# Attention slots regrouped by output batch, with the division of the results moved into attention (decoder layer, fp32, one core)

## The chip, the cores and the metric

The kernel runs on one core of a Trainium2 chip. The metric is the device time of one execution in microseconds (us). The core has five engines with a queue each: TensorE (PE in the rows; its weight loads are PEld), VectorE (DVE), ScalarE (ACT), GpSimd (POOL) and SyncE (SP), which here issues all DMA transfers. Sixteen DMA engines carry them. TensorE's clock has two levels, 2.4 GHz (1.0 in the rows) and 1.2 GHz (0.5).

## The reference

Three post-normalised blocks on x of shape (4, 1024, 512). Only the first is touched by the change:

```python
q = _lin(_lin(x, wq_w, wq_b), vq_w, vq_b)      # k and v likewise
q = q.reshape(b, s, hc, H).transpose(2, 0, 1, 3)   # 32 heads of width 16
scores = jnp.einsum('cbqh,cbkh->cbqk', q, k) / scale
attn = jax.nn.softmax(scores, axis=-1)
o = jnp.einsum('cbqk,cbkh->cbqh', attn, v)
o = o.reshape(H, b, s, hc).transpose(1, 2, 0, 3).reshape(b, s, f)
x = _layernorm(x + _lin(o, wo_w, wo_b))
# then: x = _layernorm(x + gated_cell(conv1d(x), ctx)); x = _layernorm(x + ternary_linear(round(x)))
```

The reshape of o is a reinterpretation of memory, not a transposition back. Head c and input batch b land in output batch 2 * (c % 2) + b // 2. One output batch is therefore made of the sixteen heads of one parity and two of the four input batches, and it is complete only when all sixteen are done.

## The kernel before

All matrix products but two are made of fp32r pairs: a value is split into a high part (a cast) and a low part (value minus high part), and `product3` (L140) adds hi*hi, hi*lo and lo*hi.

**combine** (L36) multiplies the two stacked weight matrices of q, k and v. **project** (L152) goes over 8 blocks of 512 columns of x. A block has 8 tiles of q and k (128 features x 512) and 4 tiles of v. For a q/k tile ScalarE writes the high part, VectorE the low part into one of four `parts` buffers, and SyncE stores both with one DMA of 512 KB to `qk_scr` (L177). v stays in `v_sb`.

**attend** (L258) has 64 slots. A slot is one head with two input batches: `cp` counts pairs of heads, `lo` picks the head of the pair, `beta` the two batches. Per slot TensorE makes two kinds of score products. The first kind (`s1_lane`, L372) gives scores of 128 queries x 1024 keys, of which VectorE takes the row maximum (L486); there are 16 such units in a slot. GpSimd splits the maxima in two parts (`split_max`, L521, L523), and SyncE writes them as two extra rows into the q operand (`store_max`, L320). The second kind (`s2`, L391) gives transposed scores with the maximum already subtracted; ScalarE takes the exponential (L466), and `pv` (L400) multiplies by v with a column of ones beside it, so that sums come out with the results. ScalarE copies the finished slot out of PSUM (`evacuate`, L455), one copy per slot. The maxima of slot s+2 are made during slot s; before slot 0 there are 32 units of maxima alone. In the last two slots there are none.

The operands `qop` and `kop` have two buffers for a head, each with both `beta` halves. `load_op` (L301) fills a half with ten DMAs: for each of two lanes one q copy of 256 KB whose source is `broadcast_to([2, DH, 2 * S])` (L308), one of 128 KB (L310) and three k copies of 64 KB (L313). SyncE issues it when slot s has used the half, and slot s+2 needs it at its start. After it SyncE stores results and sums of the slot, eight small DMAs (L353, L356).

**finish** (L561) begins with sums of batch 0: load, reciprocal on VectorE (L1118), store, and then eight chunks of 128 features, each loaded with the reciprocals spread over its rows (L699, L702), divided by VectorE (`divide`, L1133), its high part made by ScalarE (L935) and its low part by VectorE (L1137). Then come the output projection (`wo_stage`), and for each batch a `turn` of four m steps, each of four gates with 24 convolution matmuls. The next batch's chunks are loaded, divided and split during the turn. GpSimd adds `wo_b` to x tiles (L850), makes the low parts of the convolution weights (L845) and the inverse deviations, in a fixed order. Each stage is a block of its own: the next starts when every queue, SyncE's too, has come to its end.

The order on every engine is the order in which the code is written; there is no scheduler.

Of the kernel before, what the change touches and what calls it, by code (L numbers as in the profile page):

```python
# [8 lines left out]
F32 = mybir.dt.float32  # L9
# [18 lines left out]
VW = 2 * DH  # L28
EPS = 1e-5
# [122 lines left out]
def project(nc, mem, x, x_t, w_hi, w_lo, qk_bias, v_bias, qk_scr, v_sb):  # L152
# [3 lines left out]
    with ExitStack() as ctx:  # L156
# [11 lines left out]
        bank = mem["banks"]  # L168
        with nc.Block() as block:
            @block.sync  # L170
            def _(sp):
                def blocks(it, more):
                    for i in range(2):
                        for j in range(2 * KC):

                            sp.wait_ge(qk_lo, (it * 2 + i) * (2 * KC) + j + 9)
# [3 lines left out]
                        if more:  # L180

                            sp.wait_ge(x_made, it * 2 + i + 1)
                            load_x_block(sp, x, x_t, i, it * (2 * HALF) + (i + 2) * HALF)

                with sp.Fori(0, BLK // 2 - 1) as it:
                    blocks(it, True)
                blocks(BLK // 2 - 1, False)
                for i in range(4):
                    sp.wait_ge(stored[i], DMA * (BLK * 2 + 1))
# [30 lines left out]
            def _(act):  # L220
                act.sem_inc(qk_lo, 8)  # L221
                with act.Fori(0, BLK // 2) as it:
                    for i in range(2):
                        for j in range(2 * KC):
                            act.wait_ge(proj, (it * 2 + i) * GROUPS + j + 1)
                            act.wait_ge(stored[j % 4], ((it * 2 + i) * 2 + j // 4 + 1) * DMA)
# [4 lines left out]
            def _(dve):  # L231
# [4 lines left out]
                def block_of(it, i, more):  # L236
                    for j in range(2 * KC):
                        dve.wait_ge(qk_hi, (it * 2 + i) * (2 * KC) + j + 1)
# [3 lines left out]
                    for j in range(2 * KC, GROUPS):  # L242
                        dve.wait_ge(proj, (it * 2 + i) * GROUPS + j + 1)
                        nc.vector.tensor_tensor(
                            v_sb[:, bass.ds(it * (2 * KC) + (i * KC + j - 2 * KC), 1), :].rearrange("p a f -> p (a f)"),
                            bank[6 + j % 2], v_bias[:], ALU.add).then_inc(v_out, 1)
                    if more:

                        split_x_block(nc, dve, x, i, it * 2 + i + 2, it * DMA + 2 * DMA)

                with dve.Fori(0, BLK // 2 - 1) as it:
                    for i in range(2):
                        block_of(it, i, True)
                for i in range(2):
                    block_of(BLK // 2 - 1, i, False)


def attend(nc, mem, qk_scr, v_sb, o_scr, d_scr):  # L258

# [8 lines left out]
    DEEP = 4  # L268
    with ExitStack() as ctx:
        sb = lambda name, shape, dt: ctx.enter_context(nc.sbuf_tensor(name, shape, dt))  # L270
        sem = lambda name: ctx.enter_context(nc.semaphore(name))
        qop = [sb(f"q_op{i}", [P, B, S], F32R) for i in range(2)]
        kop = [sb(f"k_op{i}", [P, B, HALF], F32R) for i in range(2)]
        vop = [sb(f"v_op{i}", [P, B * QT, VW], F32) for i in range(2)]
        probs = [sb(f"probs{i}", [P, TILES, HALF], F32) for i in range(DEEP)]
        u = [sb(f"out{i}", [P, HALF], F32) for i in range(2)]
        mx = [sb(f"neg_max{b}", [P, QT], F32) for b in range(B)]
        mparts = [[sb(f"neg_max_parts{i}{b}", [P, PARTS, QT], F32R) for b in range(B)] for i in range(2)]
# [3 lines left out]
        pv_bank = bank[7]  # L282

        op_in = [[sem(f"op_in{i}{beta}") for beta in range(2)] for i in range(2)]
        max_in = [[sem(f"max_in{i}{b}") for b in range(B)] for i in range(2)]
# [11 lines left out]
        u_stored = [sem(f"u_stored{i}") for i in range(2)]  # L297

        LAST = HEADS // 2 - 1

        def load_op(sp, head, i, beta):  # L301
            cols = slice(beta * 2 * S, (beta + 1) * 2 * S)
            rows = bass.ds(head * DH, DH)
            bs = slice(2 * beta, 2 * beta + 2)
            s = op_in[i][beta]
            for lane in range(2):
                r0 = LANE * lane
                sp.dma_start(qop[i][r0:r0 + 2 * DH, bs, :].bitcast(F32),  # L308
                             qk_scr[0, 0:1, rows, cols].broadcast_to([2, DH, 2 * S])).then_inc(s, DMA)
                sp.dma_start(qop[i][r0 + 2 * DH:r0 + 3 * DH, bs, :].bitcast(F32), qk_scr[0, 1, rows, cols]).then_inc(s, DMA)  # L310
                for r, part in enumerate((0, 1, 0)):
                    k = qk_scr[1, part, rows, cols].rearrange("r (b l n) -> r b l n", b=2, l=2)[:, :, lane, :]
                    sp.dma_start(kop[i][r0 + r * DH:r0 + (r + 1) * DH, bs, :].bitcast(F32), k).then_inc(s, DMA)  # L313
        OPS = 10 * DMA

        def store_max(sp, i, b):
            for lane in range(2):
                for part in range(PARTS):
                    r = LANE * lane + ROWS + part
                    sp.dma_start(qop[i][r:r + 1, b, :].bitcast(F32),  # L320
                                 mparts[i][b][:, part, :].bitcast(F32)).then_inc(max_in[i][b], DMA)
        MAXES = 2 * PARTS * DMA
# [1010 lines left out]
```

## Time and profile before

| | us |
|---|---|
| median of 3 runs (lowest, highest) | 2441.18 (2429.57, 2443.71) |
| profiled execution, its own time | 2461.73 |
| its span | 2460.0 |
| TensorE busy | 2247.7 (91%) |
| VectorE busy | 1703.3 (69%) |
| ScalarE busy | 1397.9 (57%) |
| GpSimd busy | 431.2 (18%) |
| mean granted clock of TensorE | 0.931 |

The page divides the span in 40 slices of 61.5 us. Projection lies in slices 1 to 5, attention in slices 6 to 29, the last stage in slices 30 to 39. TensorE's busy time is no measure of need: matmuls overlap in it and its length depends on the clock. So the rows to read are those that show a wait, a clock or a place on the time line.

### The profile page before, as it was taken

How to read it: one execution, taken by the hardware profiler on the slowest of the kernel's cores; microseconds unless marked ns; L12 is line 12 of the kernel's file. 1: busy time of each engine (PE TensorE's matmuls, PEld its weight loads, DVE VectorE, ACT ScalarE, POOL GpSimd, SP SyncE). 2: the span in 40 equal slices, each digit the busy share in tenths (PEclk: the TensorE clock that was granted, in tenths of full speed). 3: DMA queues.
4: the chain of work that ended last, by engine and by line, in shares of the span. 5: the costliest groups of instructions: out<-in, count | busy, mean ns of one | idle time of the engine just before them, and what ended most of it. 6: DMA issues, size and time to landing. Idle time of an engine off the chain costs nothing. (4 is left out here: it accounts for less than half of the span.)

```text
span 2460.0 us, 41952 instructions
## 1 busy us (share of the span) xinstructions
PE 2247.7 (91%) x11688; PEld 1273.4 (52%) x11688; DVE 1703.3 (69%) x1742; ACT 1397.9 (57%) x2534; POOL 431.2 (18%) x814
## 2 busy tenths in 40 slices
PE   8999966999999999999999999999974989989896
PEld 4688843444444444444444444444413767766663
DVE  3333327888888888888888888888704666757565
ACT  0111101777787778777777777778742544444343
POOL 0000000000000000000000000000003575665754
PEclk9899985999999999999999999999957999999998
DMA  3344431222222222222222222222106544535331
GB/s 141 112 153 162 153 98 49 57 61 61 65 63 63 57 60 66 65 64 64 56 63 62 61 61 60 60 63 64 33 23 206 175 149 135 182 124 167 103 123 48
DMA packets 174858, 223.42 MB, mean 91 GB/s; under 512 B 93264, under 2 KB 94288, under 8 KB 168656
## 3 DMA queue, kind: packets, MB, share of 16 engines
q1 hardware_dynamic: 174800, 222.70, 31.2%
q8 instruction: 30, 0.49, 0.1%
q14 instruction: 28, 0.23, 0.0%
HBM read 169.12 MB, written 51.38 MB: 90 GB/s over the span
## 5 line engine op out<-in xcount | busy, mean ns | idle before, releaser
L486 DVE TENSOR_REDUCE neg_max<-psum 128x1 f32<-128x1024 f32 x1024 | 1204.7, 1219 | 214.9 <-PE psum L372 214.5
L466 ACT ACTIVATE probs<-psum 128x512 f32<-128x512 f32 x2048 | 1066.2, 605 | 409.2 <-PE psum L391 403.8
L391 PE MATMUL psum<-q_op,k_op 50*128 50x512 f32 x2048 | 776.6, 467 | 42.4 <-DMA k_op<-qk_parts_dram 29.9
L391 PEld LDWEIGHTS psum<-q_op,k_op 50*128 50x128 f32 x2048 | 362.3, 199 | 649.6 <-ACT probs L466 563.6
L372 PE MATMUL psum<-k_op,q_op 48*128 48x512 f32 x2048 | 641.0, 497 | 36.2 <-DMA k_op<-qk_parts_dram 26.3
L400 PE MATMUL psum<-probs,v_op 128*32 128x512 f32 x4096 | 574.0, 634 | 0.1
L372 PEld LDWEIGHTS psum<-k_op,q_op 48*128 48x128 f32 x2048 | 390.1, 316 | 70.2 <-issue 27.6
L521 POOL CAST neg_max_parts<-neg_max 128x8 fp32r<-128x8 f32 x128 | 24.3, 190 | 1271.2 <-DVE neg_max L486 1271.2
L147 PE MATMUL psum<-x_hi,conv_w_hi 128*128 128x512 f32 x512 | 210.1, 410 | 7.6 <-DVE x_lo L1141 7.6
L147 PE MATMUL psum<-x_lo,conv_w_hi 128*128 128x512 f32 x512 | 204.6, 400 | 0.0
L147 PE MATMUL psum<-x_hi,conv_w_lo 128*128 128x512 f32 x512 | 204.5, 399 | 0.0
L845 POOL TENSOR_TENSOR conv_w_lo<-conv_w_raw,conv_w_hi 128x1024 fp32r<-128x1024 f32 x64 | 153.6, 2402 | 115.2 <-ACT conv_w_hi L931 114.9
L400 PEld LDWEIGHTS psum<-probs,v_op 128*32 128x32 f32 x4096 | 82.1, 109 | 133.9 <-issue 58.0
L227 ACT ACTIVATE qk_parts<-psum,qk_bias 128x512 fp32r<-128x512 f32 x64 | 44.0, 688 | 166.1 <-PE psum L147 166.0
L239 DVE SCALAR_TENSOR_TENSOR qk_parts<-psum,qk_bias,qk_parts 128x512 fp32r<-128x512 f32 x64 | 48.1, 751 | 119.9 <-ACT qk_parts L227 119.9
L939 ACT ACTIVATE x<-y,neg_mean_rstd,rstd 128x512 f32<-128x512 f32 x64 | 52.2, 816 | 138.0 <-POOL neg_mean_rstd L840 138.0
L147 PEld LDWEIGHTS psum<-x_hi,conv_w_hi 128*128 128x128 f32 x512 | 99.1, 193 | 33.5 <-DVE x_lo L1141 8.8
L147 PEld LDWEIGHTS psum<-x_lo,conv_w_hi 128*128 128x128 f32 x512 | 99.0, 193 | 22.9
L1194 DVE TENSOR_TENSOR gate_in<-psum,gate_in 128x512 f32<-128x512 f32 x64 | 44.1, 690 | 95.5 <-PE psum L147 95.2
L147 PEld LDWEIGHTS psum<-x_hi,conv_w_lo 128*128 128x128 f32 x512 | 97.8, 191 | 23.2
L147 PE MATMUL psum<-x_hi,w_hi 128*128 128x512 f32 x256 | 102.2, 399 | 5.0 <-ACTq L221 5.0
L147 PE MATMUL psum<-x_lo,w_hi 128*128 128x512 f32 x256 | 101.9, 398 | 0.0
(96 smaller groups left out, 1809.1 us busy)
## 6 DMA issues: line engine op xcount, KB each, us to landing
qk_parts_dram<-qk_parts SPq DMA_DIRECT2D x64, 512.0 KB, 2.8
q_op<-qk_parts_dram SPq DMA_DIRECT2D x128, 256.0 KB
conv_w_raw<-in_conv_w_dram SPq DMA_DIRECT2D x64, 512.0 KB, 3.3
k_op<-qk_parts_dram SPq DMA_DIRECT2D x384, 64.0 KB
q_op<-qk_parts_dram SPq DMA_DIRECT2D x128, 128.0 KB
gate_in<-in_ctx_dram SPq DMA_DIRECT2D x64, 256.0 KB, 3.6
x_block<-in_x_t_dram SPq DMA_DIRECT2D x8, 1024.0 KB, 5.8
q_op<-neg_max_parts SPq DMA_DIRECT2D x512, 4.0 KB, 2.3
```

What stands on the lines that cost most here:

```text
L147: mm = nc.tensor.matmul(out, left, right, start=(first and i == 0), stop=(last and i == n - 1))
L227: nc.scalar.activation(parts[j % 4][:, 0, :], bank[j % 6], ACT.Identity, bias=qk_bias[:, j // KC, j % KC:j % KC + 1]).then_inc(qk_hi, 1)
L239: nc.vector.scalar_tensor_tensor(out=parts[j % 4][:, 1, :], in0=bank[j % 6], scalar=qk_bias[:, j // KC, j % KC:j % KC + 1], in1=parts[j % ...
L372: return nc.tensor.matmul(s1_bank[t % 2][:, lane * HALF:(lane + 1) * HALF], qop[i][r, b, t:S:QT], kop[i][r, b, :], start=True, stop=True)
L391: nc.tensor.matmul(s2_bank[cell % RING], kop[lo][r, b, n // 2 * P:(n // 2 + 1) * P], qop[lo][r, b, j % 2 * HALF:(j % 2 + 1) * HALF], start ...
L400: mm = nc.tensor.matmul(pv_bank[32 * j:32 * j + 32, :], vop[k // 2][:, (2 * (k % 2) + j // 2) * QT + kt, :], probs[n % DEEP][:, j, :], sta ...
L466: nc.scalar.activation(probs[n % DEEP][:, j, :], s2_bank[cell % RING], ACT.Exp, scale=SCALE).then_inc(exp_done, 1)
L486: nc.vector.tensor_reduce(mx[b][:, t:t + 1], s1_bank[t % 2][:], AX_X, ALU.max, negate=True).then_inc(maxed, 1)
L521: nc.gpsimd.tensor_copy(out[:, 0, :], m[:]).then_inc(split_step, 1)
L845: G.tensor_tensor(cwl[i % 4][:], raw[i % 2][:], cwh[i % 4][:].bitcast(F32), ALU.subtract).then_inc(w_lo, 1)
L939: A.activation(dst, y[r][:], ACT.Identity, bias=nmr[:, r:r + 1], scale=rstd[:, r:r + 1]).then_inc(normed, 1)
L1194: V.tensor_tensor(gin[g][:], bank[2 + g], gin[g][:], ALU.add).then_inc(gate_in, 1)
```

## The change

- Slots are numbered by output batch: slot s is head parity and half of the batches s // 16, head pair s % 16. The weights are permuted on the way in (`by_parity`), and v is stored in slot order.
- `project` writes q and k rows as the operands need them, the doubled part twice: three DMAs of 256 KB for a tile, each 8 slots x 16 rows x 512.
- `attend` has four operand buffers of one slot each. `load_op` is four DMAs of 48 rows. The load for slot s+3 is issued at the start of slot s and first needed in the middle of slot s+1. Maxima run 24 units ahead, not 32, and there are two buffers of them, not four.
- Results are stored with one DMA a slot. For every pair of slots SyncE loads sums and results back, VectorE makes the reciprocals, SyncE stores them and loads them spread over the rows, and GpSimd multiplies, casts and subtracts (`normalise`); SyncE stores the two parts.
- In the last slot SyncE loads the output projection weights and the 16 tiles of batch 0, high and low. They lie over `v_sb`. `finish` has only the last pair to divide. The tiles of later batches are loaded ready-made during the turns.

```diff
-                            sp.dma_start(
-                                qk_scr[j // KC, :, (j % KC) * P:(j % KC + 1) * P, bass.ds(it * (2 * HALF) + i * HALF, HALF)]
-                                .rearrange("a f n -> f a n"), parts[j % 4][:].bitcast(F32)).then_inc(stored[j % 4], DMA)
...
+                        for r, part in enumerate((0, 0, 1) if j < KC else (0, 1, 0)):
+                            sp.dma_start(rows[:, r, :, :], parts[j % 4][:, part, :].bitcast(F32))\
+                                .then_inc(stored[j % 4], DMA)
...
+            q = qk_scr[0, bass.ds(s * ROWS, ROWS), :].rearrange("r (b n) -> r b n", b=2)
+            k = qk_scr[1, bass.ds(s * ROWS, ROWS), :].rearrange("r (b l n) -> r b l n", b=2, l=2)
             for lane in range(2):
-                r0 = LANE * lane
-                sp.dma_start(qop[i][r0:r0 + 2 * DH, bs, :].bitcast(F32),
-                             qk_scr[0, 0:1, rows, cols].broadcast_to([2, DH, 2 * S])).then_inc(s, DMA)
...
+                rows = slice(LANE * lane, LANE * lane + ROWS)
+                sp.dma_start(qop[i][rows, :, :].bitcast(F32), q).then_inc(op_in[i], DMA)
+                sp.dma_start(kop[i][rows, :, :].bitcast(F32), k[:, :, lane, :]).then_inc(op_in[i], DMA)
...
+                    if k % 2 == 1 and not (first and k == 1):
+                        normalise(pool, nc, norm, it * 2 + (k - 3) // 2)
+                    if not (last and k >= 2):
+                        split_max((k + 2) % 4, 0, s * 2 + 4, s * 16 + LEAD + 16, it * MAXES + MAXES + DMA)
...
+def load_pair(sp, norm, us_scr, t):
+
+    for i in range(2):
+        sp.wait_ge(norm["u_stored"][i], (t + 1) * DMA + DMA)
+    sp.sem_inc(norm["waited"], 1)
+    rows = us_scr.rearrange("s (j r) n -> (s j) r n", r=VW)[bass.ds(t * 8, 8), :, :]
+    sp.dma_start(norm["sums"][:], rows[:, DH:DH + 1, :].rearrange("a o (h m) -> a (o h) m", m=VW))\
+        .then_inc(norm["sums_in"], DMA)
+    sp.wait_ge(norm["lo_made"], t + 1)
+    sp.sem_inc(norm["waited"], 1)
+    sp.dma_start(norm["o"][:], rows[:, 0:DH, :]).then_inc(norm["o_in"], DMA)
...
+def normalise(pool, nc, norm, t):
+
+    pool.wait_ge(norm["o_in"], t * (2 * DMA) + 2 * DMA)
+    nc.gpsimd.tensor_tensor(norm["o"][:], norm["o"][:], norm["den"][:], ALU.mult).then_inc(norm["o_made"], 1)
...
+def load_o(sp, late, on_scr, b, n):
+
+    i, c = n // KC, n % KC
+    for part, dst in enumerate((late["o_hi"], late["o_lo"])):
+        src = on_scr[part].rearrange("(h l q) n -> h l q n", l=2, q=VW)[bass.ds(b * 16 + c * 4, 4), i, :, :]
+        sp.dma_start(dst[:, n, :].bitcast(F32), src).then_inc(late["o_in"][i], DMA)
...
-                            if g == 2 and m < KC - 1 and not last:
-                                for n in (2 * m + 2, 2 * m + 3):
-                                    next_o(b + 1, n)
+                            if g == 2 and not last:
+                                for n in (2 * m, 2 * m + 1):
+                                    load_o(sp, late, on_scr, b + 1, n)
```

How the queues change at three places. SyncE in the projection, two q/k tiles, before:

```order
39 L177 ISA
40 L177 DMA qk_parts_dram<-qk_parts 128x2x512
41 L176 REGISTER_ALU
42 L177 ISA
43 L177 DMA qk_parts_dram<-qk_parts 128x2x512
```

and after:

```order
34 L187 DMA qk_parts_dram<-qk_parts 8x16x512
35 L187 DMA qk_parts_dram<-qk_parts 8x16x512 x2
36 L187 DMA qk_parts_dram<-qk_parts 8x16x512
37 L187 DMA qk_parts_dram<-qk_parts 8x16x512 x2
...
```

One store for a tile has become three, and their first dimension is 8.

SyncE in the loop of attention, one operand load (`q_op`, `k_op`) with what follows it, before:

```order
125 L308 ISA
126 L308 DMA q_op<-qk_parts_dram 32x1x2048
127 L310 ISA
128 L310 DMA q_op<-qk_parts_dram 16x2048
129 L313 ISA
130 L313 DMA k_op<-qk_parts_dram 16x2x512
131 L313 ISA
132 L313 DMA k_op<-qk_parts_dram 16x2x512 x2
133 L308 DMA q_op<-qk_parts_dram 32x1x2048
134 L310 DMA q_op<-qk_parts_dram 16x2048
```

and after, in a slot that also stores the two parts and reads the next pair back (`attended_dram` holds results with their sums):

```order
...
117 L306 ISA
118 L306 DMA q_op<-qk_parts_dram 48x2048
119 L307 ISA
120 L307 DMA k_op<-qk_parts_dram 48x2x512
121 L306 DMA q_op<-qk_parts_dram 48x2048
122 L307 ISA
123 L307 DMA k_op<-qk_parts_dram 48x2x512
124 L338 ISA
125 L313 DMA q_op<-neg_max_parts 1x128x8 x4
```

The copies of 32, 16 and 16 rows are one of 48 rows, and they stand ahead of the maxima of the next slot, no longer behind both of them.

GpSimd in the loop of attention, from one split of maxima to the next, before:

```order
46 L521 CAST neg_max_parts<-neg_max 128x8
47 L522 REGISTER_ALU
48 L523 TENSOR_TENSOR neg_max_parts<-neg_max,neg_max_parts 128x8
49 L516 ISA
50 L521 CAST neg_max_parts<-neg_max 128x8
51 L522 REGISTER_ALU
52 L523 TENSOR_TENSOR neg_max_parts<-neg_max,neg_max_parts 128x8
```

and after:

```order
55 L535 CAST neg_max_parts<-neg_max 128x8
56 L536 ISA
57 L537 TENSOR_TENSOR neg_max_parts<-neg_max,neg_max_parts 128x8
58 L617 ISA
59 L618 TENSOR_TENSOR o_raw<-o_raw,recips 128x512
60 L620 ISA
61 L622 CAST o_parts<-o_raw 128x512
62 L624 TENSOR_TENSOR o_parts<-o_raw,o_parts 128x512
63 L530 REGISTER_ALU
64 L535 CAST neg_max_parts<-neg_max 128x8
```

The three wide operations stand between two splits in every second slot.

## Rows read from the trace of the kernel before

**Rows 1.** The page's 40 slices: TensorE busy, its clock (tenths), DMA share.
```profile
PE   8999966999999999999999999999974989989896
...
PEclk9899985999999999999999999999957999999998
DMA  3344431222222222222222222222106544535331
```

**Rows 2.** Waits of TensorE, 400 to 1760 us: total us, times, longest.
```profile
PE psum L391 <- DMA k_op<-qk_parts_dram: 29.9, 32, 1.6
```

**Rows 3.** Time line of ScalarE, copies of slots 0, 27, 28, 61 and 63.
```profile
441.73 0.58 ACT L455 COPY out<-psum 128x512 f32<-128x512 f32 x1
...
1030.91 0.58 ACT L455 COPY out<-psum 128x512 f32<-128x512 f32 x1
...
1051.82 0.58 ACT L455 COPY out<-psum 128x512 f32<-128x512 f32 x1
...
1773.93 0.58 ACT L455 COPY out<-psum 128x512 f32<-128x512 f32 x1
...
1835.18 0.58 ACT L455 COPY out<-psum 128x512 f32<-128x512 f32 x1 [3.00 <-PE psum L400]
```

**Rows 4.** Stretches: busy PE, PEld, DVE, ACT, POOL; clock, DMA share, GB/s.
```profile
1327.00:1335.00 8.00, 6.39 (x34) 2.71 (x32) 4.82 (x5) 4.24 (x8) 0.39 (x2) 0.73 0.12 25
1030.90:1051.80 20.90, 20.90 (x130) 9.62 (x128) 18.84 (x17) 17.00 (x34) 0.79 (x4) 1.00 0.26 65
```

**Rows 5.** Stretches for the DMA engines, columns as in rows 4.
```profile
204.00:206.00 2.00, 2.00 (x10) 1.64 (x9) 0.69 (x1) 0.00 (x0) 0.00 (x0) 1.00 1.03 386
903.00:909.00 6.00, 6.00 (x41) 3.06 (x39) 5.28 (x5) 4.82 (x11) 0.00 (x0) 1.00 0.56 122
...
915.00:918.00 3.00, 3.00 (x21) 1.37 (x24) 2.74 (x3) 2.45 (x6) 0.00 (x0) 1.00 0.13 55
```

**Rows 6.** Time line, projection's first store and entry into attention.
```profile
81.65 1.77 SPq L177 DMA_DIRECT2D qk_parts_dram<-qk_parts  x2
...
346.19 1.76 DVE L479 MEMSET k_op<- 128x2048 f32 x1 [0.89 <-PEq L169]
...
366.94 4.48 SPq L313 DMA_DIRECT2D k_op<-qk_parts_dram  x3
370.84 1.25 PE L372 MATMUL psum<-k_op,q_op 48*128 48x512 f32 x4 [26.27 <-DMA k_op<-qk_parts_dram]
...
371.70 36.29 DVE L486 TENSOR_REDUCE neg_max<-psum 128x1 f32<-128x1024 f32 x32 [20.52 <-PE psum L372]
...
413.32 0.76 PE L391 MATMUL psum<-q_op,k_op 50*128 50x512 f32 x1 [6.73 <-DMA q_op<-neg_max_parts]
```

**Rows 7.** Groups by line, VectorE: busy us, mean ns, idle before.
```profile
L1229 DVE RECIPROCAL x_int<-x_int 128x256 f32<-128x256 f32 x3 | 5.0, 1713 | 0.0
```

**Rows 8.** VectorE's reductions, line 486: ns, lowest, median, highest.
```profile
L486 DVE TENSOR_REDUCE neg_max<-psum x1024: 1209/1216/1226, 371.7 to 1769.6; 128x1 f32<-128x1024 f32 x171
```

**Rows 9.** Stretch of the last two slots, columns as in rows 4.
```profile
1774.00:1835.00 61.00, 57.29 (x185) 14.58 (x185) 0.00 (x0) 31.49 (x62) 0.00 (x0) 0.50 0.02 5
```

**Rows 10.** Time line, GpSimd and TensorE at the start of the last stage.
```profile
1882.02 4.76 POOL L845 TENSOR_TENSOR conv_w_lo<-conv_w_raw,conv_w_hi 128x1024 fp32r<-128x1024 f32 x2 [23.91 <-ACT conv_w_hi L931]
1886.73 0.20 POOL L903 COPY x<-z0s 128x8 f32<-128x8 f32 x1
...
1907.50 0.80 PE L147 MATMUL psum<-x_hi,conv_w_hi 128*128 128x512 f32 x1 [7.63 <-DVE x_lo L1141]
```

**Rows 11.** Last stage: a wait, two groups, one DMA issue (median us to landing).
```profile
PE psum L1048 <- ACT x_int_t L949: 57.0, 11, 11.4
...
L1133 DVE TENSOR_TENSOR o_raw<-o_raw,recips 128x512 f32<-128x512 f32 x24 | 15.4, 683 | 0.0
...
L935 ACT CAST o_hi<-o_raw 128x512 fp32r<-128x512 f32 x24 | 13.5, 609 | 0.0
...
x_wo<-in_x_dram SPq DMA_DIRECT2D x20, 256.0 KB, 2.7
```

More of the change, by code:

```diff
@@ L360, in _ @@
+                for k in range(4):
+                    slot(0, k, first=True)
+                with sp.Fori(1, LAST) as it:
                     for k in range(4):
-                        slot(cp, k, True)
+                        slot(it, k)
                 for k in range(4):
-                    slot(LAST, k, False)
-                for i in range(2):
-                    sp.wait_ge(u_stored[i], HEADS * 8 * DMA + DMA)
-            U_STORE = 8 * DMA
+                    slot(LAST, k, last=True)
@@ L414, in slot @@
                             unit = 2 * n + half
+                            ahead = k + 1 if unit < QT else k + 2
                             for side in range(2):
@@ L502, in _, with slot @@
-                with dve.Fori(0, LAST) as cp:
-                    for k in range(4):
-                        slot(cp, k)
-                for k in range(2):
-                    slot(LAST, k)
+                for n in range(LEAD):
+                    if n == 16:
+                        dve.wait_ge(split, 1)
+                    maxima(n // QT % 2, n % QT, n)
+                def slot(it, k, first=False, units=16):
+                    s = it * 4 + k
+                    for n in range(units):
+                        if n % QT == 0:
+                            dve.wait_ge(split, s * 2 + n // QT + 2)
+                        if n == 2 and k % 2 == 1 and not (first and k == 1):
+                            recips(dve, nc, norm, it * 2 + (k - 3) // 2)
+                        maxima(1 - n // QT, n % QT, s * 16 + n + LEAD)
@@ new lines, in _ @@
+                for k in range(4):
+                    slot(0, k, first=True)
+                with dve.Fori(1, LAST) as it:
+                    for k in range(4):
+                        slot(it, k)
+                slot(LAST, 0)
+                slot(LAST, 1)
+                slot(LAST, 2, units=QT)
+                recips(dve, nc, norm, PAIRS - 2)
+                dve.wait_ge(late["wo_in"], DMA)
+                nc.vector.tensor_copy(late["wo_hi"][:], late["x2"][:, 0:KC, :]).then_inc(late["wo_hi_made"], 1)
@@ new lines, in _, with store_out @@
+                for k in range(4):
+                    slot(0, k, first=True)
+                with pool.Fori(1, LAST) as it:
+                    for k in range(4):
+                        slot(it, k)
+                for k in range(4):
+                    slot(LAST, k, last=True)
+def store_out(sp, norm, us_scr, s, i):
+    sp.dma_start(us_scr[bass.ds(s, 1), :, :].rearrange("s p n -> p (s n)"), norm["u"][i][:])\
+        .then_inc(norm["u_stored"][i], DMA)
+def load_pair(sp, norm, us_scr, t):
+    for i in range(2):
+        sp.wait_ge(norm["u_stored"][i], (t + 1) * DMA + DMA)
[6 more added lines that the diff above has]
+    sp.dma_start(norm["o"][:], rows[:, 0:DH, :]).then_inc(norm["o_in"], DMA)
@@ L775, in turn @@
                         if m == 0 and not last:
-                            for n in range(2):
-                                next_o(b + 1, n)
+                            sp.wait_ge(row_full, wo_row(b, first) + TT)
+                            sp.wait_ge(norm["parts_stored"], (PAIRS + 1) * DMA)
+                            sp.sem_inc(waited, 1)
                         if not first:
@@ L987, in turn @@
                                 A.activation(tc[:], cell[:], ACT.Tanh).then_inc(tanh_made, 1)
-                            if g == 2 and not last:
-                                for j in range(2):
-                                    hi_o(b + 1, 2 * m + j)
                             if g == 2 and m < KC - 1 and not first:
@@ L1198, in turn @@
                                     rounded(b, 2 * m - 2 + j, before + j)
-                            if g == 1 and not last:
-                                for j in range(2):
-                                    divide(b + 1, 2 * m + j)
                             if g == 2:
```

481 lines of the change are left out of this document (232 added, 249 removed).

## The prediction

> **What bounds the kernel now.** I read the page's slices first: TensorE is busy nearly everywhere, so I look for where its clock is low and where it is empty. [rows 1] show two such places, around slice 6 (entry into attention) and slices 29 and 30 (from attention to the last stage), and small dents in the clock all through attention. Next the waits of TensorE inside attention: 30 waits, 29.9 us, for k_op [rows 2]. What they do to a slot is seen from ScalarE's copy of the result, one in each of the 64 slots: two successive copies lie 20.91 us apart where nothing was waited for, but the first and the 62nd lie 1332.2 us apart, 21.84 us a slot [rows 3]. So 61 slots lose 0.93 us each, 57 us: 30 are the waits themselves, the rest is the half clock that follows a wait, as at 1327 to 1335 us, where the granted clock averages 0.73, against 1.00 in the undisturbed slot [rows 4].
>
> Why the load is late shows in the DMA share. While many transfers run, the 16 engines are busy at 1.03 with 386 GB/s; in the tail of each operand load the share is 0.13 with 55 GB/s [rows 5]. 0.13 of 16 is two engines. The tail is the q copy whose source is written with a leading dimension of 2. From these two ends (leading dimension 2: two engines; 128: all) I take it that **a transfer gets as many engines as its leading dimension has steps**, at 386/16 = 24.1 GB/s each, and that they are always the same first ones. The sum rests on this: the change removes the leading 2, but adds transfers with a leading 8 and 4.
>
> The Trainium skill (DMA: Bandwidth & Descriptors, Why a DMA increments its semaphore by 16 and not by 1) gives the same as a rule: the largest number up to 16 that divides the slowest dimension of both sides, on the lowest-numbered engines. It speaks against two of the new transfers; the trace agrees at leading dimension 2 and has no clean stretch for 8 or 4.
>
> **The change, part by part** (against the profiled execution, 2461.73 us, span 2460.0).
>
> *Projection.* Each of 64 q/k tiles is now stored three times 256 KB, as 8x16x512, instead of once 512 KB over 128 partitions. On eight engines (193 GB/s) 0.786 MB take 4.07 us; TensorE makes 96 tiles, 32 of them v tiles that are not stored, in the 264.5 us from the first store to the next stage, 2.8 us each. So stores set the pace: 64 x 4.07 = 261 us plus six x blocks of 1 MB at 2.7 us is 277 us. The first store is at 81.65, so the last lands near 361, where attention began at 346.19 [rows 6]: **+14 us**. Bounds: 0 if all 16 engines serve them (131 us, hidden), +25 if a crowded engine is slower than 24.1 GB/s.
>
> *Entry into attention.* Before, 67.1 us pass from 346.19 to the first score matmul of the second kind (413.32); the first one of the first kind waits until 370.84, and SyncE itself is held up in issuing (4.48 us for three small DMAs) because two engines have a queue [rows 6]. Now one operand set is 1.18 MB in four transfers of 48 rows, three sets 3.5 MB, 9 us at 386 GB/s. Memsets and the first landing take about 6 us, then 24 units of maxima instead of 32, at 36.29/32 = 1.13 us: 27.1 us. 33 instead of 67: **-34 us**. The maxima of slot 0 are stored by unit 20, so that last wait goes too. Bounds -25 and -36.
>
> *Steady slots.* A load (3 us on 16 engines) now has one and a half slots, 31 us, so both the waits and the dents behind them go: -57. New in the slots: every second slot a reciprocal of 32 columns on VectorE (256 columns took 1.71 us [rows 7], so about 0.3; VectorE idles 0.25 us a pair of units, part shows): +3. GpSimd's three 128x512 operations, some 3.5 us, lie in the 10 us between two splits of maxima; VectorE's reduction reads PSUM and varies only from 1209 to 1226 ns [rows 8] with GpSimd's copies beside it, so I charge nothing for them. VectorE has now two maxima buffers, not four: it waits for a split made half a slot earlier. **-54 us**, bounds -10 and -57.
>
> *Last slots.* Without maxima the clock falls to 0.50 and the last two slots take 61.2 us [rows 3, 9]. Half a slot of that runs at full rate now, 10.5 instead of 15.3: **-5 us**.
>
> *Seam.* Before: 71.7 us from the last copy's end (1835.76) to the first convolution matmul at 1907.50 [rows 3, 10]. Now output projection weights and all of batch 0 are requested in slot 63, about 24 us before attention ends. But these are 16 transfers of 256 KB with leading dimension 4: 4.19 MB on four engines (96.5 GB/s) are 43.5 us, with the weights 46. SyncE can hardly run ahead of its queue (the 4.48 us above), so its last store and the end of the stage come some 22 us after TensorE is done: the early load is only half early. In the next stage: sums of the last pair issued after eight DMAs and landed (9 us), reciprocal, store, recips load (to 15 us), GpSimd's three operations (to 19), two conv_w_lo at 2.4 (to 24). From that point, where GpSimd copies z0, it was 20.8 us to the convolution [rows 10]; constants now go ahead of it, so 18. Together 22 + 42 = 64 against 71.7: **-7 us**. Bounds: -28 (loads on all engines) and +25.
>
> *Last stage.* VectorE loses 24 divisions and 24 subtractions of 0.7 us, ScalarE 24 copies of 0.61 [rows 11]. In turn 0 they were under the convolution; in turns 1 and 2 part of the 57.0 us that TensorE waits for ScalarE's x_int_t goes, but the large ones (the longest 11.4 us) follow the output projection, which GpSimd paces. I take -6 (bounds 0 and -15). Against it: four loads per m step, 1.05 MB on four engines, 10.9 us. At the end of a turn x tile 4 queues behind them; landed 2.7 us after its issue before [rows 11], it comes about 5 us late, and GpSimd must add it before it goes on. Three turns: +15. **+9 us**, bounds -10 and +40.
>
> Sum: 14 - 34 - 54 - 5 - 7 + 9 = **-77 us**, 2385 in the profiled frame. The profiled run is 20.5 us above the median of 2441.18. If all of that were waits for loads, unprofiled runs have less to regain, -57; I take the middle, -66: **2375 us**, own range 2340 to 2410.
>
> **Rivals.**
> *B, the other dimension decides and the loads spread.* All these transfers have 128 partitions on one side. For it: a full share at most times; against it: the 0.13 tail. Then projection +0, seam -28, last stage -6: 50 us less, 2325.
> *C, the wait moves.* GpSimd's division waits for the reciprocals on its queue ahead of the next split of maxima, and that split holds VectorE and then TensorE. Its chain (store, sums, reciprocal, store, load, each 2 to 3 us) has to end by about 17 us of the slot; I find it at 11 to 15. If it misses, every second slot loses more than 1 us and the clock dents with it, and 44 of the 54 stay: 2419.
> *D, slower.* The engines do less than 24.1 GB/s each when transfers mix. At 903 to 909 us it is 122 GB/s at a share of 0.56, 13.6 GB/s per busy engine [rows 5]. Then batch 0 needs 77 us (+34), and an m step (96 convolution matmuls at 0.22 us, 21 us in turn 0, some 29 in the later turns with the ternary product and its waits) needs 19.3 for its four loads, 9.6 for weights and 4.8 for ctx on the first four engines, 34 in all: +52 in turn 0, +44 in turns 1 and 2, less the 9 already counted: 2496. It decides from about 17 GB/s per engine downwards. Against it: those are 2 KB and 8 KB pieces crowded on two engines, not an even load.
>
> **How the numbers follow.** Forecast 0.57, B 0.13, C 0.17, D 0.08, other mishaps 0.05. The predicted time is the forecast's. The range 2312 to 2430 takes in B and C and leaves out D. One per cent (24 us) is about what a measurement can tell from no change: faster by more holds the forecast, B and half of C, 0.78; the rest of C and a bit of each, 0.12; slower D and mishaps, 0.10.
>
> **What would show it.** Right: no wait for k_op in attention, copies 20.9 to 21.0 us apart, first score matmul of attention some 6 us after the stage's start; q/k stores at a share near 0.5 without pauses up to 360; in the last slot and after it a share near 0.25, TensorE idle some 65 us; GpSimd waiting for x tiles at each end of a turn. Wrong: a share near 1 in those stretches (B); VectorE or TensorE waiting for GpSimd's splits every second slot (C); TensorE waiting for conv_w or o_hi inside the turns (D).

## The result, and the profile after

The changed kernel takes 2476.51 us (median of 4 runs, 2471.38 to 2478.00) beside 2439.53 for the kernel before (2429.57 to 2443.71). The ratio is 1.0154, 95% interval [1.0119, 1.0189]: slower by 1.5%, where 2375 was forecast. The profiled execution took 2477.05 us with a span of 2475.3; before, the span was 2460.0. The spans differ by 15.3 us and the medians by 37.0, because the profiled execution before (2461.73) lay 22 us above its median. The table splits the 15.3 us, a sum of large amounts of both signs; the forecast in the same frame was -77. The stretches end at the same rows in both traces:

| stretch, us | before | after | difference | forecast |
|---|---|---|---|---|
| start to attention's first memset | 346.2 | 399.2 | +53.0 | +14 |
| to the first score matmul of the second kind | 67.1 | 37.1 | -30.0 | -34 |
| to the first copy of a result | 28.4 | 27.1 | -1.3 | |
| first to 62nd copy | 1332.2 | 1281.1 | -51.1 | -54 |
| 62nd to last copy | 61.2 | 49.3 | -11.9 | -5 |
| last copy's start to the first convolution matmul | 61.7 | 52.9 | -8.8 | -7 |
| to the end | 563.1 | 628.6 | +65.5 | +9 |

One bound has to be put right. The prediction took the matmul at 1907.50 in [rows 10] for the first of the convolution. It is the first behind a gap; twelve stand ahead of it. TensorE's time line of the kernel before, where they begin:

```profile
1896.67 0.39 PE L147 MATMUL psum<-wo_hi,o_lo 128*128 128x512 f32 x1
1896.90 0.40 PE L147 MATMUL psum<-x_hi,conv_w_hi 128*128 128x512 f32 x1
```

and the same place after:

```profile
1846.70 0.77 PE L149 MATMUL psum<-x_hi,conv_w_hi 128*128 128x512 f32 x1 [11.73 <-DVE x_lo L1158]
```

So the seam before was some 61 us long, not 71.7. The table uses 1896.90.

**What went as forecast.** TensorE waits for no k_op in attention's slots any more, and the copies stand 1281.1 us / 61 = 21.00 us apart. ScalarE's time line, copies 1, 62 and 64, against [rows 3]:

```profile
463.37 0.58 ACT L457 COPY out<-psum 128x512 f32<-128x512 f32 x1
...
1744.46 0.58 ACT L457 COPY out<-psum 128x512 f32<-128x512 f32 x1
...
1793.79 0.59 ACT L457 COPY out<-psum 128x512 f32<-128x512 f32 x1 [2.60 <-PE psum L403]
```

**What did not: the projection.** Before, TensorE was never held there behind the first store. The groups of waits from 80 to 400 us after (in each row: who waits, for whom, us in total, times, longest):

```profile
DVE qk_parts L245 <- ACT qk_parts L232: 134.1, 40, 7.4
ACT qk_parts L232 <- DMA qk_parts_dram<-qk_parts: 111.1, 27, 10.8
...
DVE x_hi L136 <- DMA x_block<-in_x_t_dram: 47.1, 6, 10.5
PE psum L149 <- DVE values L251: 35.0, 6, 8.5
```

The stores do run on eight DMA engines: busy share 0.53 and 204 GB/s in a stretch of stores alone, 25.5 GB/s an engine, so a q/k tile of 0.786 MB takes 3.85 us. But a little later the DMA engines carry nothing at all (share 0.00). Windows (columns as in [rows 4]):

```profile
310.00:318.00 8.00, 7.60 (x23) 6.05 (x24) 1.63 (x3) 0.00 (x0) 0.00 (x0) 0.67 0.53 204
...
326.00:330.00 4.00, 4.00 (x19) 3.22 (x18) 3.44 (x3) 1.02 (x2) 0.00 (x0) 1.00 0.00 1
```

The time line of SyncE and of VectorE from the last stores of one block to the first of the next shows why:

```profile
313.39 4.85 SPq L187 DMA_DIRECT2D qk_parts_dram<-qk_parts  x4
318.29 1.14 SPq L129 DMA_DIRECT2D x_block<-in_x_t_dram  x1
330.77 3.30 SPq L187 DMA_DIRECT2D qk_parts_dram<-qk_parts  x4
```

```profile
326.52 1.23 DVE L136 CAST x_hi<-x_block 128x2048 fp32r<-128x2048 f32 x1 [7.36 <-DMA x_block<-in_x_t_dram]
327.79 2.29 DVE L138 TENSOR_TENSOR x_lo<-x_block,x_hi 128x2048 fp32r<-128x2048 f32 x1
330.00 2.72 DVE L245 SCALAR_TENSOR_TENSOR qk_parts<-psum,qk_bias,qk_parts 128x512 fp32r<-128x512 f32 x4
```

The x block load is issued behind the block's last store (318.29), VectorE waits for it (326.52), splits it, and only then makes the low part that the next store needs (330.77). A round takes 41.4 us; TensorE needs 33.6 for a block. Before the change a round took just these 33.6 us, as SyncE's x block loads show:

```profile
201.26 0.39 SPq L127 DMA_DIRECT2D x_block<-in_x_t_dram  x1
...
234.90 0.39 SPq L127 DMA_DIRECT2D x_block<-in_x_t_dram  x1
```

**And the last stage.** Waits from 1846 us to the end, after the change:

```profile
POOL conv_w_lo L884 <- ACT conv_w_hi L971: 134.6, 26, 13.0
...
ACT conv_w_hi L971 <- DMA conv_w_raw<-in_conv_w_dram: 51.3, 9, 10.0
...
PE psum L149 <- DMA o_lo<-attended_parts_dram: 48.2, 3, 23.1
```

In the kernel before, ScalarE waited 0.5 us in all for these weights (from 1896 us to the end):

```profile
ACT conv_w_hi L931 <- DMA conv_w_raw<-in_conv_w_dram: 0.5, 1, 0.5
```

SyncE's time line after the change around the four new loads of an m step:

```profile
1880.00 0.33 SPq L775 DMA_DIRECT2D conv_w_raw<-in_conv_w_dram  x1
1880.37 0.57 SPq L633 DMA_DIRECT2D o_hi<-attended_parts_dram  x1
1880.99 0.55 SPq L633 DMA_DIRECT2D o_lo<-attended_parts_dram  x1
1881.58 0.54 SPq L633 DMA_DIRECT2D o_hi<-attended_parts_dram  x1
1882.16 0.56 SPq L633 DMA_DIRECT2D o_lo<-attended_parts_dram  x1
1882.77 3.17 SPq L771 DMA_DIRECT2D gate_in<-in_ctx_dram  x1
1885.99 0.58 SPq L775 DMA_DIRECT2D conv_w_raw<-in_conv_w_dram  x1
```

Ctx and weights are issued behind the burst, and SyncE itself is held 3.17 us at the ctx load. At the end of turn 0 TensorE stands idle for the last of them, at half clock, with some four engines busy (0.28 of 16) and 101 GB/s. The three waits for `o_lo`, one at the end of each turn, come to 48.2 us, beside the 65.5 lost. Its time line and a window of that stretch:

```profile
1987.70 0.80 PE L149 MATMUL psum<-wo_hi,o_hi 128*128 128x512 f32 x1 [23.07 <-DMA o_lo<-attended_parts_dram]
```

```profile
1982.00:1987.00 5.00, 0.00 (x0) 0.00 (x0) 1.57 (x3) 1.43 (x2) 0.05 (x1) 0.50 0.28 101
```

### The profile page after: what moved, and what is told of

It reads as the page before. It is cut to its first block, busy times and chain, and to the rows that moved or that the text cites. A ratio compares the mean times of both kernels' runs of the same rounds, so it can differ in the third digit from the quotient of the medians.

```text
span 2475.3 us, 40345 instructions
## 1 busy us (share of the span) xinstructions
PE 2235.3 (90%) x11688; PEld 1280.1 (52%) x11688; DVE 1676.5 (68%) x1709; ACT 1378.2 (56%) x2501; POOL 524.2 (21%) x942
## 2 busy tenths in 40 slices
DMA packets 204432, 281.64 MB, mean 114 GB/s; under 512 B 95441, under 2 KB 95441, under 8 KB 198225
## 4 chain that ended last, share of the span: by engine, by line
PE 58%; issue 8%; POOL 7%; DMA 4%; DVE 3%; SPq 2%; ACT 1%; POOLq 0%; DVEq 0%; ACTq 0%
PE psum L394 23%; PE psum L403 20%; PE psum L376 10%; PE psum L149 4%; POOL conv_w_lo L884 3%; DMA conv_w_raw<-in_conv_w_dram 2%; SPq L633 2%; POOL rstd L877 1%; DVE neg_max L488 1%; POOL x L894 1%; DMA x_wo<-in_x_dram 1%; PE psum L1077 1%; POOL x_wo L889 1%; DMA attended_dram<-out 1%; POOL var_eps L874 1%
## 5 line engine op out<-in xcount | busy, mean ns | idle before, releaser
L468 ACT ACTIVATE probs<-psum 128x512 f32<-128x512 f32 x2048 | 1065.7, 605 | 319.1 <-PE psum L394 318.9
L394 PE MATMUL psum<-q_op,k_op 50*128 50x512 f32 x2048 | 760.7, 453 | 5.1 <-ACT probs L468 4.3
L394 PEld LDWEIGHTS psum<-q_op,k_op 50*128 50x128 f32 x2048 | 356.0, 193 | 588.0 <-ACT probs L468 571.5
L376 PE MATMUL psum<-k_op,q_op 48*128 48x512 f32 x2048 | 629.5, 487 | 24.1 <-DMA k_op<-qk_parts_dram 16.6
L403 PE MATMUL psum<-probs,v_op 128*32 128x512 f32 x4096 | 552.7, 612 | 1.5
L525 POOL COPY v_op<-values 128x256 f32 (+1 forms) x64 | 25.4, 397 | 509.0 <-issue 399.2
L971 ACT CAST conv_w_hi<-conv_w_raw 128x1024 fp32r<-128x1024 f32 x64 | 66.5, 1039 | 91.2 <-DMA conv_w_raw<-in_conv_w_dram 91.2
L149 PE MATMUL psum<-wo_hi,o_hi 128*128 128x512 f32 x128 | 53.5, 418 | 65.8 <-DMA o_lo<-attended_parts_dram 48.2
```

What stands on the lines that cost most here:

```text
L149: mm = nc.tensor.matmul(out, left, right, start=(first and i == 0), stop=(last and i == n - 1))
L376: return nc.tensor.matmul(s1_bank[t % 2][:, lane * HALF:(lane + 1) * HALF], qop[i][r, b, t:S:QT], kop[i][r, b, :], start=True, stop=True)
L394: nc.tensor.matmul(s2_bank[cell % RING], kop[i][r, j // 2, n // 2 * P:(n // 2 + 1) * P], qop[i][r, j // 2, j % 2 * HALF:(j % 2 + 1) * HALF ...
L403: mm = nc.tensor.matmul(pv_bank[32 * j:32 * j + 32, :], vop[k % 2][:, j // 2 * QT + kt, :], probs[n % DEEP][:, j, :], start=(n == 0), stop ...
L468: nc.scalar.activation(probs[n % DEEP][:, j, :], s2_bank[cell % RING], ACT.Exp, scale=SCALE).then_inc(exp_done, 1)
L971: A.copy(cwh[i % 4][:], raw[i % 2][:]).then_inc(w_hi, 1)
```

## The experiments

The theory at first: the losses of these two stages come from transfers confined to eight and to four DMA engines by their leading dimension. The rival: they come from the added bytes (281.64 MB instead of 223.42) or the added DMAs, whatever the engines. Stages of the profiled runs, in us, with bounds as above (seam: 62nd copy to the first convolution matmul). Each ratio is to runs of the kernel before taken beside that kernel; their medians lie between 2432.93 and 2442.77 us, so times of different rows are compared by the ratios and the stages.

| kernel | ratio to before, 95% | first store to attention | to first copy | 61 slots | seam | last stage |
|---|---|---|---|---|---|---|
| before | 1 | 264.6 | 95.5 | 1332.2 | 123.0 | 563.1 |
| after | 1.0154 [1.0119, 1.0189] | 319.0 | 64.2 | 1281.1 | 102.2 | 628.6 |
| e1 stores 16 | 0.9921 [0.9898, 0.9944] | 264.5 | 64.4 | 1280.3 | 104.1 | 625.8 |
| e2 loads 16 | 0.9722 [0.9677, 0.9766] | 318.9 | 64.4 | 1281.0 | 74.5 | 554.3 |
| e3 both | 0.9510 [0.9464, 0.9556] | 264.4 | 66.8 | 1281.0 | 81.7 | 547.9 |
| e4 before, q 16 | 0.9761 [0.9693, 0.9828] | 264.6 | 79.4 | 1277.2 | 114.9 | 562.3 |
| e5 v between | 1.0143 [1.0076, 1.0210] | 315.3 | 65.4 | 1280.9 | 102.8 | 622.9 |
| e6 one a gate | 0.9922 [0.9889, 0.9956] | 318.2 | 65.6 | 1280.8 | 101.8 | 559.0 |
| e9 x early | 0.9983 [0.9954, 1.0013] | 268.9 | 65.5 | 1280.9 | 104.9 | 625.9 |
| e10 both orders | 0.9723 [0.9670, 0.9775] | 270.6 | 64.4 | 1280.0 | 102.8 | 565.9 |
| e11 all | 0.9508 [0.9468, 0.9549] | 264.4 | 64.2 | 1279.9 | 71.2 | 553.8 |

**e1, stores on 16 engines.** The weights of q and k are permuted (not shown) so that a tile's features are numbered row first, slot second.

```diff
-                            .rearrange("(s r d) n -> s r d n", r=3, d=DH)
+                            .rearrange("(s r d) n -> d r s n", r=3, d=DH)
```

> The changed kernel with one edit: the 128 features of a q/k tile are permuted by the weights, so that each store's leading dimension is 16 and not 8; bytes, number of stores and their order stay. Theory (the projection is slow because 8 of 16 DMA engines carry the stores): the stores show a share near 1, attention's first memset comes near 347 us again instead of 399, and the time falls by some 45 to 2430 us (ratio to the kernel before 0.997). Rival (three stores a tile and their bytes cost that much on any number of engines): the stage keeps most of its 47 to 53 us and the time stays within 15 of 2476.

2422.06 us (8 runs). The stage is as long as before the change, to 0.1 us, with one and a half times the stored bytes. TensorE waits for nothing in it. A window of it:

```profile
270.00:278.00 8.00, 8.00 (x36) 6.46 (x35) 2.46 (x4) 0.00 (x0) 0.00 (x0) 1.00 0.92 277
```

On 16 engines bytes and number of stores cost nothing; the rival is out for the projection.

**e2, loads on 16 engines.** The rows of the output projection's weights are permuted alike (not shown).

```diff
-        src = on_scr[part].rearrange("(h l q) n -> h l q n", l=2, q=VW)[bass.ds(b * 16 + c * 4, 4), i, :, :]
+        src = on_scr[part].rearrange("(h l q) n -> h l q n", l=2, q=VW)[bass.ds(b * 16 + c * 4, 4), i, :, :]\
+            .rearrange("h q n -> q h n")
```

> The changed kernel with one edit: the tiles of the output projection are loaded with their 32 rows ahead of the 4 heads (the output projection's weights permuted alike), so that the leading dimension is 32 and not 4. Theory (the four engines that carry these loads delay convolution weights, ctx and x tiles behind them): the waits for o_lo (48 us) and most of the 91 us that ScalarE waits for conv_w_raw go, the last stage falls from 629 to some 555, the seam from 52 to some 35: 2476 - 74 - 17 = 2385 (0.978). Rival (the order of SyncE's queue and the added 12.6 MB do it, whatever the engines): at most 20 us of the last stage come back, 2440 to 2460.

2373.41 us (4 runs). The last stage gives back 74.3 us, as expected, and the seam 27.7, more than the 17 expected. (The 91 us named there are ScalarE's waits for these weights with the seam; the last stage has 51.3 of them.) ScalarE no longer waits for conv_w_raw at all in the last stage, and TensorE's waits for o_lo are 2.3 us. The added bytes are out here too; the order of SyncE's queue, which the rival in the expectation names beside them, is taken up in e6.

**e3, both.**

> The two edits (stores with leading dimension 16, loads with 32) together. Theory: both gains add, 2476 - 45 - 91 = 2340 (0.959). If instead one loss hides the other (the stage that is freed gets a new wait), less than 110 of the 136 us come: above 2366.

2321.48 us (4 runs, 2317.42 to 2325.14), 155 below the changed kernel: the gains of e1 (54) and e2 (103) add, and both were larger than expected.

**e4, the kernel before with the q copy on 16 engines.**

```diff
-                sp.dma_start(qop[i][r0:r0 + 2 * DH, bs, :].bitcast(F32),
-                             qk_scr[0, 0:1, rows, cols].broadcast_to([2, DH, 2 * S])).then_inc(s, DMA)
+                for r in range(2):
+                    sp.dma_start(qop[i][r0 + r * DH:r0 + (r + 1) * DH, bs, :].bitcast(F32),
+                                 qk_scr[0, 0, rows, cols]).then_inc(s, DMA)
```

> The kernel before with one edit: the q load whose source is a broadcast with leading dimension 2 is two loads of 16 rows, same bytes, 12 DMAs an operand load instead of 10. Theory (two DMA engines carry that copy, and this alone makes TensorE wait in the slots): no waits for k_op in attention, slots 20.9 to 21.0 us apart, entry a few us shorter, the time 50 to 65 lower, 2375 to 2390 (0.975 to 0.98). Rival (the waits need the earlier issue and the four buffers, because a load of 1 MB also stands behind the maxima and the result stores in SyncE's queue): most of the 30 waits stay, the time falls by less than 20.

2386.58 us (4 runs, 2368.47 to 2390.14). The slots are 20.94 us apart. All that TensorE's matmuls still wait for between 420 and 1760 us:

```profile
PE psum L392 <- ACT probs L467: 5.3, 16, 0.5
```

So the whole gain of the change in the steady slots, and more (1277.2 beside 1281.1), comes from this one line. Four buffers, three slots of maxima ahead and the earlier issue are not needed for it.

**e5, v tiles between the q/k tiles.** With 16 engines (e1) the stage is 54 us shorter, but eight tiles at 3.85 us are 31 us, less than TensorE's 33.6. What holds the stage then? First guess: the four v tiles at the end of a block. TensorE and VectorE now take them in between:

```diff
+    ORDER = (0, 1, 8, 2, 3, 9, 4, 5, 10, 6, 7, 11)
...
-                        for j in range(GROUPS):
+                        for j in ORDER:
```

> The changed kernel with one edit: in each block of the projection a v tile stands behind every second q/k tile on TensorE and VectorE, where all four v tiles stood at the end; the stores stay on eight engines. Theory (a block takes 41 us because the store queue runs dry while VectorE and TensorE are held at the v tiles, and fills again too late: eight tiles at 3.84 us are 31 us and would fit into TensorE's 33 us): the DMA queue no longer runs dry, the 35 us that TensorE waits for VectorE's values go, attention starts 40 to 50 us earlier than at 399, and the time is about 2432 us. Rival (eight engines bound the stage in any order, x block loads and slower packets included): 25 us or more of the 53 stay, 2450 or above.

2471.84 us: nothing, so this guess falls. TensorE's waits for v fell from 35.0 to 8.5 us, but 19.3 us of waits for VectorE's q/k parts are new, and VectorE's waits for the x block grew from 47.1. Their group from 80 to 420 us:

```profile
DVE x_hi L136 <- DMA x_block<-in_x_t_dram: 90.1, 6, 16.1
```

The rival's number came true but not its reason (e9), since the queue still stood empty once a block. This pointed at the loop of SyncE, x block and VectorE told above.

**e6, one load behind each gate,** on four engines as in the changed kernel:

```diff
-                            if g == 2 and not last:
-                                for n in (2 * m, 2 * m + 1):
-                                    load_o(sp, late, on_scr, b + 1, n)
+                            if not last:
+                                load_o(sp, late, on_scr, b + 1, 2 * m + g // 2, (g % 2,))
```

The last argument picks the high or the low part.

> The changed kernel with one edit: in the turns the four loads for the output projection of an m step are issued one behind each gate instead of four behind the third gate; they stay on four engines with the same bytes. Theory (a burst: 10.4 us of queue on four engines in one piece stands ahead of convolution weights that have only two raw buffers and ahead of ctx, while the mean load of these engines, 18 us in an m step of 21 or 29, would fit): the wait of TensorE for o_lo and of ScalarE for conv_w_raw shrink to less than half and the last stage loses 40 to 60 of its 76 us: 2420 to 2435. Rival (throughput: four engines carry more than they can in a turn, order is nothing): at most 25 us come back, above 2450.

2414.66 us (10 runs). The last stage is 559.0 us: 69.6 of the 74.3 that 16 engines give back come from the order alone, and TensorE's waits for `o_lo` fall from 48.2 to 18.1 us. ScalarE's group of waits from 1846 us, 51.3 in the changed kernel:

```profile
ACT conv_w_hi L971 <- DMA conv_w_raw<-in_conv_w_dram: 5.0, 5, 1.8
```

Four engines can carry the turns. What they can't do without holding the others up is carry 1.05 MB, 10.4 us at 101 GB/s, in one piece ahead of weights with two buffers.

**e7 and e8, what makes operand loads slow.** Both on e3, one execution each. e7:

```diff
-                sp.dma_start(qop[i][rows, :, :].bitcast(F32), q).then_inc(op_in[i], DMA)
+                for b in range(2):
+                    for c in (slice(0, HALF), slice(HALF, S)):
+                        sp.dma_start(qop[i][rows, b, c].bitcast(F32), q[:, b, c]).then_inc(op_in[i], DMA)
```

> The kernel with both edits (stores 16, loads 32), and q operands loaded as four DMAs of 48 rows x 2 KB instead of one of 48 rows x 8 KB; same bytes, ten DMAs a slot instead of four. In that kernel the first 384 KB q copy after an empty queue takes some 2.7 us on all 16 engines (147 GB/s). If the 8 KB piece is what is slow, the first operand set lands some 3 us earlier than 10 us after its issue and the three sets are 10 us shorter in all; if the piece's size is nothing, the set takes as long or longer (SyncE's issue of 0.6 us each then counts). Attention's steady slots stay at 21.0 us either way.

> The kernel with both edits, and 512 bytes of padding behind each 8 KB row of the scratch in DRAM. If rows that lie a multiple of 8 KB apart collide in memory, operand loads get faster (a set of four in less than 5 us instead of 7.5) and the entry into attention shorter by some 5 us; if not, nothing moves.

In e8 the scratch has `2 * S + 128` columns. They took 2319.83 and 2313.12 us beside e3's 2321.48; from a single execution neither can be told from e3. 15 us of the entry's loads in e3, in e7 and in e8 (windows, the last two columns are DMA share and GB/s):

```profile
348.00:363.00 15.00, 6.51 (x18) 2.77 (x18) 8.41 (x8) 0.00 (x0) 0.00 (x0) 0.50 1.04 158
```

```profile
354.00:369.00 15.00, 7.15 (x20) 2.94 (x20) 9.37 (x9) 0.00 (x0) 0.06 (x1) 0.50 1.07 180
```

```profile
350.00:365.00 15.00, 6.16 (x16) 2.45 (x16) 8.40 (x10) 0.00 (x0) 0.00 (x0) 0.50 1.05 170
```

Smaller pieces give 14% more GB/s and padding 8%; TensorE's first wait shrinks from 12.2 to 11.3 and 11.8 us, where 3 us (e7) and some 5 (e8) had been expected if they were the cause. Neither is the main cause: the 16 engines are still busy and still move less than half of the 386 GB/s in [rows 5].

**e9, the x block load earlier.**

```diff
-                    if blk + 2 < BLK:
-
-                        sp.wait_ge(x_made, blk + 1)
-                        load_x_block(sp, x, x_t, i, (blk + 2) * HALF)
+                        if j == 3 and blk + 2 < BLK:
+                            sp.wait_ge(x_made, blk + 1)
+                            load_x_block(sp, x, x_t, i, (blk + 2) * HALF)
```

> The changed kernel with one edit: in the projection SyncE issues the load of the next but one x block behind the fourth of the eight q/k tiles, not behind the eighth; the stores stay on eight engines. Interleaving v tiles had moved nothing, and the trace shows a closed loop of 41.4 us a block: 28.7 us from the first to the last tile's stores on SyncE, 8.4 for the x block behind them, and 4.3 until VectorE, which splits that block before its next q/k tile, has let the first store go again. Theory (that loop): VectorE's 90 us of waits for x_block go, a block takes 33.6 to 35 us, attention starts at 350 to 362 instead of 399 and the time falls by some 40 to 2436. Rival (eight engines cannot carry it: 8 x 3.84 + 2.6 for the x block are 33.3 us against TensorE's 33.6, and mixing makes it more): a block takes 37 us or more, and less than half comes back, above 2455.

(The 90 us named there are those of e5; in the changed kernel they are 47.1, and 35.0 more stand in TensorE's waits for v.) 2429.83 us (10 runs): 50.1 of the 54.5 us of the stage come back with the stores still on eight engines, and VectorE waits for no x block. TensorE never stops; a window of it over 40 us, share 0.52, then SyncE's stores without a pause in the same time:

```profile
290.00:330.00 40.00, 40.00 (x173) 32.19 (x172) 10.62 (x15) 6.88 (x10) 0.00 (x0) 1.00 0.52 197
```

```profile
289.45 41.71 SPq L187 DMA_DIRECT2D qk_parts_dram<-qk_parts  x31
```

The loop is shown, and the rival (too few engines in any order) is out but for the last 4.4 us.

**e10, both orders, and e11, everything.**

> Both orders in the changed kernel: the x block load earlier, and one load for the output projection behind each gate. All stores and loads stay on eight and four engines. If the losses are waits behind bursts in SyncE's queue, both gains add: 2476 - 40 - 62 = 2374 (0.972). If the number of engines counts by itself, more than 2390.

> Stores on 16 engines and loads on 16, both orders, and the padded rows. Where the engines are 16 the orders should give nothing more, since neither loop is near the bound any longer (projection 264 us from the first store, as before; last stage 546 us): 2313 to 2322, ratio 0.951. If the orders matter there too, 2305 or less.

e10 takes 2365.29 us (4 runs), e11 2316.94 (6 runs). Both orders add, as forecast, without one engine more. With 16 engines the orders and the padding give nothing that can be told from e3 (0.9508 beside 0.9510). What e10 lacks against e11 is 6 us in the projection, 12 in the last stage and 32 in the seam: SyncE must have issued batch 0's 4.19 MB on four engines before attention's stage can end, and no order of the turns touches that.

**The last slots differ between kernels whose attention code is the same.** From the 62nd to the last copy, the changed kernel and e10:

```profile
1744.50:1793.80 49.30, 44.91 (x195) 12.99 (x193) 10.55 (x9) 31.50 (x63) 3.54 (x5) 0.72 0.27 93
```

```profile
1694.00:1733.40 39.40, 34.03 (x195) 10.70 (x193) 10.62 (x9) 31.50 (x63) 3.56 (x5) 1.00 0.28 91
```

In e10 and e11 the clock stays at 1.00 to the end; in the changed kernel it falls to 0.50 on the way. With the loads on four engines these 9.9 us buy nothing: TensorE then stands idle longer before the output projection (17.11 us in the changed kernel, 27.05 in e10), and the seam is 102.2 and 102.8 us.

e3 or e11, 4.9% faster than the kernel before, is the version to keep.

## Why the prediction was wrong

*What bounds the kernel.* Right, and with the right reason. "A transfer gets as many engines as its leading dimension has steps" is borne out at 4 (0.28 of 16 with 101 GB/s) and 8 (0.53 with 204 GB/s), at 2 by e4, where the waits go with the leading 2, and e1 and e2 remove the losses by that dimension alone. That the engines are always the same first ones is not shown. Rival B, which denied the rule, is out. The rule of the Trainium skill (DMA: Bandwidth & Descriptors, Why a DMA increments its semaphore by 16 and not by 1), which spoke against two of the new transfers, was right on both, by the two shares just given.

*Projection, +14 and measured +53: the step that failed* is "so stores set the pace: 64 x 4.07 = 261 us plus six x blocks", a sum of the DMA queue's own busy time. The stores were quicker than that (3.85 us), but the queue did not stay full: the x block load is behind the last store on SyncE, VectorE splits it ahead of its next q/k tile, and no store can be issued meanwhile. Before the change the same loop fitted into TensorE's 33.6 us (201.26 to 234.90). The change lengthened one member of it and thereby made it the bound (e9, with e5 as the check that it was not the v tiles).

*Last stage, +9 and measured +65.5: the second step that failed.* I asked what queues behind the loads only at the end of a turn (x tile 4, 5 us). Behind each burst also stand, at every m step, ctx and the next convolution weights, which have two raw buffers; they come late, ScalarE, GpSimd and TensorE follow. Rival D had these queues, and its place and sign are right. Its premise, "the engines do less than 24.1 GB/s each when transfers mix", is seen too. The four engines moved 101 GB/s, 25 each, when little else ran, but behind a burst, with weights and ctx in the queue, it is 195 GB/s at a share of 0.82, 15 for each busy engine:

```profile
1884.00:1894.00 10.00, 10.00 (x45) 8.08 (x44) 3.13 (x6) 4.19 (x6) 4.36 (x2) 1.00 0.82 195
```

What cost the time was nevertheless the burst: e6 gets nearly all back on the same four engines with the same bytes. Scaled to 24.1 GB/s, rival D's own 34 us are 19 in an m step of 21, and on that I held the case improbable; a mean says nothing of a wait behind one long piece. Rival D's time, 2496, came nearest to the measured one, partly by luck: it has 34 us in the seam that did not come, and leaves out the projection's loss.

*Entry, -34 and measured -30.* Mechanism right. The first set landed later than assumed: TensorE's wait ended at 409.78, 10.6 us behind the memset at 399.22, where I had 6. The loads were charged at 386 GB/s; from 405 to 420 us they move 163 at a share of 1.05.

*Steady slots, -54 and measured -51.1.* Right in size. The term for VectorE's reciprocal and the rest, 3 us, came out as 1281.1 against 61 x 20.91 = 1275.5: 5.6; of what it is made was not tested. Rival C (the wait moves to GpSimd) is out: the 61 copy intervals lie between 20.96 and 21.46 us, and GpSimd's split never holds TensorE for the microsecond or more every second slot that it asked.

*Last slots and seam, -12 and measured -20.7.* The early load was, as forecast, only half early: e2 shows that four engines cost 28 us here. The rest is luck. The step "without maxima the clock falls to 0.50" did not hold for the whole of the last slots (0.72 on average, and 1.00 in e10), and with that go their -11.9. For the seam itself the sum said 64 us against a row of 71.7, and it was 52.3 against 61.1: two errors of some 11 us that cancel. TensorE did not stand idle for some 65 us either, but for 17.11 before the output projection and 11.73 before the convolution.

*The forecast's frame.* The chance of 0.08 for slower was too small. The halved credit for the frame, -66 for -77, is small beside these misses. Each of the two failed steps took an added transfer and priced its own length, without writing down who waits in the same queue behind it every round.

## What to carry to other kernels

Look at the leading dimension of every new transfer first; a permutation of weights can often make it 16, here for 155 us. Then, for each transfer that gets longer or is added, follow one whole round of the queue that issues it: what stands behind it, which engine waits in order for that, and what this engine must do before the queue can go on. If the round is longer than the bounding engine's, it is the bound, however idle the DMA engines look; moving one load earlier in the queue or spreading a burst then gives nearly as much as more engines (50.1 of 54.5 and 69.6 of 74.3 us here), but not where one large load as a whole must be through, as in the seam.

## What the runs showed of the hardware

Loads of 48 rows keep all 16 engines busy (share 1.04) at only 158 GB/s in e3, beside 386 in [rows 5]; e7 and e8 move that to 180 and 170. In the entry of e4, where all operand loads have 16 rows, it is 131 GB/s at the same share. What limits them stays open: loads that write more partitions were not tried.

Eight engines reach 204 GB/s and four 101 when little else runs, 25 GB/s each; in the mix behind a burst it is 15 for each busy engine. SyncE is held in issuing while the few engines of earlier DMAs are behind: 3.17 us for one ctx load behind four loads on four engines, in the rows above, and 0.42 us for the same load at 1870.68, where none stood ahead. The sixteen loads of batch 0 on four engines took SyncE from 1769.56 to 1803.43 to issue.

The last slots, the same code in both kernels, take 49.3 us at a mean granted clock of 0.72 (the changed kernel) and 39.4 at 1.00 (e10).
